# Second SAGE layer: one-hots loaded from HBM in place of made on VectorE, and stored there by the first

## The reference, cut to what matters

```
def _sage_conv(x, src, dst, Wl, Wr, b):
    msg = x[src]                                   # one row per edge
    agg = segment_sum(msg, dst)                    # summed by target node
    agg = agg / maximum(cnt, 1.0)
    return agg @ Wl.T + x @ Wr.T + b
h = relu(bn(sage_conv(x, src, dst, Wl0, Wr0, b0))) # first layer  (layer 0)
h = bn(sage_conv(h, src, dst, Wl1, Wr1, b1))       # second layer (layer 1)
x = layernorm(x + h)
```

## Time and profile before

| What | us |
|---|---|
| median of 3 runs (lowest 9302.91, highest 9314.57) | 9308.34 |
| span of the profiled execution, first to last instruction | 7890.3 |
| median less span | 1418.0 |
| layer 0 of SAGE, tile loop, 5421 to 6579 in the span | 1158 |
| layer 1 of SAGE, tile loop, 6684 to 7887 in the span | 1203 |

### The profile page before, as it was taken

One profiled execution on the slowest core, in us unless ns is written; L12 is line 12 of the kernel. 1 busy time (PEld: TensorE's weight loads), 2 busy tenths in 40 slices (PEclk: granted clock), 3 DMA queues, 4 the chain that ended last, 5 costly groups with the idle time before them and its releaser, 6 DMA issues.

```text
span 7890.3 us, 195306 instructions
## 1 busy us (share of the span) xinstructions
PE 5464.8 (69%) x50500; PEld 3952.8 (50%) x50501; DVE 4825.2 (61%) x14588; ACT 3085.2 (39%) x7615; POOL 5124.5 (65%) x4726
## 2 busy tenths in 40 slices
PE   3767677777773746777776777435878874888887
PEld 3655556565651336666666666323444442444444
DVE  7555555555556556666666666575666663555555
ACT  2111111111121135555555555413555552666665
POOL 1776767676740157777777777025887784777777
PEclk9977675656555855555555555567999996999999
DMA  3223232323233532222222222033555553544444
GB/s 122 57 56 77 56 77 56 77 56 77 56 76 125 148 47 52 52 51 51 51 51 51 51 51 51 12 91 95 124 124 125 124 125 92 120 116 118 118 118 107
DMA packets 600102, 647.29 MB, mean 82 GB/s; under 512 B 331121, under 2 KB 490355, under 8 KB 599665
## 3 DMA queue, kind: packets, MB, share of 16 engines
q0 software_dynamic: 190000, 384.58, 23.9%
q1 hardware_dynamic: 338379, 238.04, 10.4%
q10 hardware_dynamic: 71640, 23.81, 1.2%
HBM read 562.39 MB, written 83.23 MB: 82 GB/s over the span
## 4 chain that ended last, share of the span: by engine, by line
DVE 27%; issue 19%; POOL 15%; DMA 14%; PE 13%; DVEq 5%; ACT 3%; SPq 3%; ACTq 1%; POOLq 0%
POOL acc L659 8%; POOL rows L639 7%; DMA acc<-list_dst 7%; PE psa L1407 4%; PE psc L1366 3%; DMA rows<-t_gat,idx 2%; DVE acc L1729 2%; DVE acc L1781 1%; DMA acc<-in_x 1%; DVEq L619 1%; DMA acc<-y_d 1%; DVE acc L1728 1%; ACT ohb L1120 1%; PE psc L1498 1%; DVE s_m L1837 1%
## 5 line engine op out<-in xcount | busy, mean ns | idle before, releaser
L639 POOL DMA_INDIRECT rows<-t_gat,idx x3168 | 3142.8, 992 | 1189.8 <-issue 903.3
L659 POOL DMA_INDIRECT acc<-t_part,acc x1400 | 1826.6, 1305 | 546.6 <-issue 460.2
L1407 PE MATMUL psa<-rhs,rows 128*128 128x176 f32 (+1 forms) x6336 | 1713.1, 431 | 23.2 <-DVEq L1922 12.2
L1217 ACT ACTIVATE acc<-psa 128x384 bf16<-128x384 f32 x3200 | 1290.2, 506 | 884.7 <-PE psa L1481 765.8
L1407 PEld LDWEIGHTS psa<-rhs,rows 128*128 128x128 f32 x6336 | 1497.2, 311 | 132.0 <-DVEq L1922 83.2
L1481 PE MATMUL psa<-den,rhs 125*32 125x384 bf16 x12800 | 785.2, 343 | 191.4 <-ACT acc L1217 149.8
L1128 ACT ACTIVATE wgt<-s_d 128x64 f32<-128x64 f32 (+1 forms) x396 | 93.8, 237 | 1625.5 <-DVE s_d L1838 1610.8
L1122 ACT ACTIVATE oht<-psc 22x1024 bf16<-22x1024 bf16 x402 | 407.3, 1013 | 783.9 <-PE psc L1366 730.4
L1395 PE MATMUL psc<-oh,wgt 128*8 128x22 f32 (+1 forms) x6336 | 290.2, 205 | 552.1 <-ACT wgt L1128 543.8
L1071 ACT ACTIVATE acc<-stg,acc 128x128 bf16<-128x128 f32 x1818 | 552.9, 387 | 198.2 <-issue 116.0
L1481 PEld LDWEIGHTS psa<-den,rhs 125*32 125x32 bf16 x12800 | 285.6, 97 | 641.9 <-ACT acc L1217 412.7
(11 more groups left out here) (348 smaller groups left out, 7870.4 us busy)
## 6 DMA issues: line engine op xcount, KB each, us to landing
rows<-list_src SPq DMA_DIRECT2D x200, 500.0 KB
rows<-t_gat,idx POOLq DMA_INDIRECT x3168
acc<-y_d SPq DMA_DIRECT2D x50, 1000.0 KB, 5.0
y_d<-stg SPq DMA_DIRECT2D x100, 250.0 KB, 2.8
acc<-t_part,acc POOLq DMA_INDIRECT x1400
acc<-t_sage SPq DMA_DIRECT2D x300, 62.5 KB
adw<-win_d SPq DMA_DIRECT2D x820, 2.2 KB
adw<-win_d SPq DMA_DIRECT2D x788, 0.4 KB
```

The source lines that it names most:

```text
L639: eng.indirect_dma_start(rows[:, j, 0:spec["width"]], None, spec["table"], bass.IndirectOffsetOnAxis(ap=idx[:, j:j + 1], axis=0)).then_inc ...
L659: eng.indirect_dma_start(h_prow[u][:, t, :], None, t_parts[layer], bass.IndirectOffsetOnAxis(ap=h_idx[u][:, t:t + 1], axis=0)).then_inc(h_ ...
L1217: eng.activation(h_rows[:, g, :], psa[:, g % 4, 0:D3], ACT.Copy).then_inc(hyb["ev"], 1)
L1407: last = eng.matmul(sums(half, q, h), rows[:, slot * TH + j, 0:D], right, start=(j == 2 * q), stop=(j == 2 * q + 1))
```

## The change

Two tensors are added in HBM, one row per tile: `onehots_d` (128 x 2875 bf16, 736,000 bytes a tile) and `fetches_d` (125 x 2048 bf16, 512,000 bytes a tile).

- In layer 0 DVE makes both one-hots as before. SP stores `oh_src` of tile t after `lists(t)` and ahead of `own(t-1)` (`fetches_out`, after a wait for `sources(t)`), and `oh_dst` of tile t-1 after `own(t-1)` (`onehots_out`). DVE waits for the store of tile k-2 to be over before it writes the same buffer again.
- In layer 1 DVE makes neither (`targets` and `sources` are not called). SP loads `oh_src` from `fetches_d` in place of `list_src`, once the gathers of tile t-2 are done on PE; it loads no `list_dst`; after `list_idx` it loads `oh_dst` from `onehots_d`, once the segment sums of tile t-2 are done. PE waits for the loads where it waited for DVE.
- SP waits at each layer's end for the moves to be over.

```diff
@@ -188,6 +188,8 @@
         list_src = dram("list_src", (NT, GP * EP), BF16)
         list_dst = dram("list_dst", (NT, EP, GT), BF16)
         list_idx = dram("list_idx", (NT, EP, TP), I32)
+        onehots_d = dram("onehots_d", (NT, EP, GT * NP_), BF16)
+        fetches_d = dram("fetches_d", (NT, NP_, GP * EP), BF16)
         win0_d = dram("win0_d", (NW, 3 * K0), BF16)
         win1_d = dram("win1_d", (NW, 3 * K1), BF16)
         bnd0_d = dram("bnd0_d", (NP_, NT * H))
@@ -479,6 +481,9 @@
                          ("turn", "at", "ht", "mps", "used"))
         h_in = {k: [sem(f"h_{k}_in{u}") for u in range(2)] for k in ("lists", "idx", "own", "rows")}
         h_out = [sem(f"h_out{u}") for u in range(2)]
+        oh_moved = [n_msg[f"in{u}"] for u in range(2)]
+        src_moved = [n_bn[f"in{u}"] for u in range(2)]
+        moved_before = [16 * ((NC + 1 - u) // 2) for u in range(2)]
         act_l = sem("act_l")
 
         block = ctx.enter_context(nc.Block())
@@ -583,6 +588,14 @@
                     step(i * 2, t)
             for t in range(4):
                 step(NT - 2, t)
+
+        def onehots_of(e, k):
+
+            return onehots_d[ds(e + k, 1), :, :].rearrange("o p n -> p (o n)")
+
+        def fetches_of(e, k):
+
+            return fetches_d[ds(e + k, 1), :, :].rearrange("o p n -> p (o n)")
 
         def there(e, k):
             return not isinstance(e, int) or 0 <= e + k < NT
@@ -893,17 +906,40 @@
 
             def lists(e, k):
                 u, before, n = k % 2, later(e, k), e + n0
-                if before:
-                    eng.wait_ge(hyb["ohs"], n + (k - 1))
-                eng.dma_start(h_src[u], list_src[ds(e + k, 1), :].to_broadcast([NP_, EP * GP])).then_inc(h_in["lists"][u], 16)
-                if before:
-                    eng.wait_ge(hyb["ohd"], n + (k - 1))
-                eng.dma_start(h_dst[u][:, 0:GT], list_dst[ds(e + k, 1), :, :].rearrange("o p t -> p (o t)")
-                              ).then_inc(h_in["lists"][u], 16)
+                if layer:
+                    if before:
+                        eng.wait_ge(hyb["gps"], n * GP + (k - 1) * GP)
+                    eng.dma_start(oh_src[u].rearrange("p g s -> p (g s)"), fetches_of(e, k)).then_inc(src_moved[u], 16)
+                else:
+                    if before:
+                        eng.wait_ge(hyb["ohs"], n + (k - 1))
+                    eng.dma_start(h_src[u], list_src[ds(e + k, 1), :].to_broadcast([NP_, EP * GP])
+                                  ).then_inc(h_in["lists"][u], 16)
+                if not layer:
+                    if before:
+                        eng.wait_ge(hyb["ohd"], n + (k - 1))
+                    eng.dma_start(h_dst[u][:, 0:GT], list_dst[ds(e + k, 1), :, :].rearrange("o p t -> p (o t)")
+                                  ).then_inc(h_in["lists"][u], 16)
                 if before:
                     eng.wait_ge(h_in["rows"][u], n * (8 * TP) + 16 * TP * (k // 2))
                 eng.dma_start(h_idx[u][:, :], list_idx[ds(e + k, 1), :, :].rearrange("o p t -> p (o t)")
                               ).then_inc(h_in["idx"][u], 16)
+
+            def onehots_in(e, k):
+                u = k % 2
+                if later(e, k):
+                    eng.wait_ge(hyb["seg"], e + (n0 + k - 1))
+                eng.dma_start(oh_dst[u].rearrange("p g n -> p (g n)"), onehots_of(e, k)).then_inc(oh_moved[u], 16)
+
+            def fetches_out(e, k):
+                u = k % 2
+                eng.wait_ge(hyb["ohs"], e + (k + 1))
+                eng.dma_start(fetches_of(e, k), oh_src[u].rearrange("p g s -> p (g s)")).then_inc(src_moved[u], 16)
+
+            def onehots_out(e, k):
+                u = k % 2
+                eng.wait_ge(hyb["ohd"], e + (k + 1))
+                eng.dma_start(onehots_of(e, k), oh_dst[u].rearrange("p g n -> p (g n)")).then_inc(oh_moved[u], 16)
 
             def own(e, k):
                 u = k % 2
@@ -916,8 +952,14 @@
             def step(e, t):
                 if there(e, t):
                     lists(e, t)
+                    if layer:
+                        onehots_in(e, t)
+                    else:
+                        fetches_out(e, t)
                 if there(e, t - 1):
                     own(e, t - 1)
+                    if not layer:
+                        onehots_out(e, t - 1)
             return step
 
         def sp_node(eng, S, first, second=None):
@@ -1045,6 +1087,10 @@
                 eng.wait_ge(sp_in, 16 * n_in[0])
                 phase_end(eng, 9 + 2 * layer)
                 by_step(eng, sp_step(eng, layer))
+                for u in range(2):
+                    for moved in (oh_moved, src_moved):
+                        eng.wait_ge(moved[u], moved_before[u] + (layer + 1) * 16 * (NT // 2))
+                        eng.sem_inc(alone, 1)
                 phase_end(eng, 10 + 2 * layer)
 
 
@@ -1473,7 +1519,9 @@
 
             def gather(e, k, g):
                 u, n = k % 2, e + n0
-                if g == 0:
+                if g == 0 and layer:
+                    eng.wait_ge(src_moved[u], e * 8 + (moved_before[u] + 16 * (NT // 2) + 16 * (k // 2 + 1)))
+                if g == 0 and not layer:
                     eng.wait_ge(hyb["ohs"], n + (k + 1))
                 if g >= 4 or there(e, k - 1):
                     eng.wait_ge(hyb["ev"], n * GP + (k * GP + g - 3))
@@ -1486,7 +1534,10 @@
             def segment(e, k, g):
                 u, n = k % 2, e + n0
                 if g == 0:
-                    eng.wait_ge(hyb["ohd"], n + (k + 1))
+                    if layer:
+                        eng.wait_ge(oh_moved[u], e * 8 + (moved_before[u] + 16 * (NT // 2) + 16 * (k // 2 + 1)))
+                    else:
+                        eng.wait_ge(hyb["ohd"], n + (k + 1))
                     if later(e, k):
                         eng.wait_ge(hyb["comb"], n + (k - 1))
                         eng.sem_inc(alone, 1)
@@ -1972,9 +2023,10 @@
 
             def sources(e, k):
                 u, n = k % 2, e + n0
-                eng.wait_ge(h_in["lists"][u], n * 16 + 32 * (k // 2 + 1))
+                eng.wait_ge(h_in["lists"][u], e * 16 + 32 * (k // 2 + 1))
                 if later(e, k):
                     eng.wait_ge(hyb["gps"], n * GP + (k - 1) * GP)
+                    eng.wait_ge(src_moved[u], e * 8 + (moved_before[u] + 16 * (k // 2)))
                     eng.sem_inc(alone, 1)
                 eng.tensor_scalar(oh_src[u].rearrange("p g s -> p (g s)"), h_src[u], node1[:, 0:1], None,
                                   ALU.is_equal).then_inc(hyb["ohs"], 1)
@@ -1986,6 +2038,7 @@
                 link(tt(h_dstm[:, 0:GT], h_dst[u][:, 0:GT], dst_off[:, 0:1].to_broadcast([EP, GT]), ALU.add))
                 if later(e, k):
                     eng.wait_ge(hyb["seg"], n + (k - 1))
+                    eng.wait_ge(oh_moved[u], e * 8 + (moved_before[u] + 16 * (k // 2)))
                     eng.sem_inc(alone, 1)
                 link(tt(oh_dst[u], iota1[:, 0:NP_].unsqueeze(1).to_broadcast([EP, GT, NP_]),
                         h_dstm[:, 0:GT].unsqueeze(2).to_broadcast([EP, GT, NP_]), ALU.is_equal))
@@ -2047,11 +2100,11 @@
                 link.end()
 
             def step(e, t):
-                if there(e, t):
+                if there(e, t) and not layer:
                     targets(e, t)
                 if there(e, t - 2):
                     turned(e, t - 2)
-                if there(e, t + 1):
+                if there(e, t + 1) and not layer:
                     sources(e, t + 1)
                 if there(e, t - 2):
                     centre(e, t - 2)
@@ -2059,7 +2112,8 @@
                         scale(e, t - 2)
                 if there(e, t - 1):
                     combine(e, t - 1)
-            sources(0, 0)
+            if not layer:
+                sources(0, 0)
             return step
 
         @block.vector
```

## The result

The changed kernel takes 10352.16 us against 9312.49 us, medians of 5 runs each: 1.112 times as long, interval 1.1106 to 1.1133, +1040 us. Forecast were 9690 us and a range up to 9960. The sign is right, the size is not.

The account below looks back on a forecast made before the run. It took each tile loop to be paced by a chain through SP's list loads and DVE's one-hots, with POOL nearly equal in layer 0. Layer 0 +502 us and layer 1 -121 us gave +381, so 9690 us, range 9440 to 9960.

Parts of the forecast that it names:

- What was shown as the base: Whole kernel: a traced span of 7890.3 us with 1418.0 us more around it, kept unchanged, from a median of 9308.34.
- Two covers go with L1990: Layer 1, targets' one-hots no longer made on DVE: PE's 0.9 us wait for `turned` and the lengthened POOL gather end.
- without it POOL needs 7 x 1.25 = 8.75 us a tile and is no bound: Layer 1: with no DVE operation stretching a gather from 0.95 to 3.15 us, POOL's seven gathers don't set the pace.
- the two stores: Layer 0, SP's queue: storing `oh_src` costs 3.85 us on five engines, storing `oh_dst` 1.73 us, ahead of the next list.
- The queue's 9.91: Layer 0, one round on SP's queue: `oh_src` store 3.85, own rows 0.48, `oh_dst` store 1.73, source list 3.85 us.
- the packets of POOL and ACT: Layer 0: other transfers sharing the DMA engines add 4.3 us to the round, between 3.0 and 5.5.
- No gain in layer 1: Rival: `oh_src` load takes the list's place, nothing won; layer 1 at 11.9 to 12.5 us, 9797 to 9856; chance 0.15.
- cheaper stores: Rival: 125-partition stores use all engines or packets fit gaps; layer 0 at 12.8 to 14.5 us, 9307 to 9473; chance 0.12.
- hidden: Rival: stores are hidden, POOL paces layer 0 at 11.58 us, only the -121 us remains, 9187; chance 0.06.
- stretched: Rival: other engines' packets grow in proportion to the transfers; layer 0 at 19.3 us a tile, 9944 in all; chance 0.12.
- the signs named: Layer 0 loop some 1660 us, DVE awaiting lists 5 us; layer 1 some 1080, POOL's mean about 0.95, PE awaiting loads.

Follow-up runs that it names:

- e0: The kernel before, unchanged, run again on a 7900 chip: 7904.8 us, ratio 1.001.
- h0: The kernel before, unchanged, one run on a 9200 chip for a trace: 9206.7 us against 9168.3.
- g2: Changed kernel, but layer 1 loads only the sources' one-hots and makes the targets' on DVE; 9200 chip: 9669.3 us, 1.055 times the kernel before.
- t1: Changed kernel, sources' one-hots split 112/13, layer 0 stores behind the next loads, useless DVE operation in layer 1; 9200 chip: 9189.9 us, 1.003.
- h1: The changed kernel, unchanged, beside the kernel before on a 9200 chip: 10222.4 us, ratio 1.115.
- g1: Changed kernel, but layer 1 loads only the targets' one-hots and makes the sources' on DVE; 9200 chip: 10220.6 us, 1.115 times the kernel before.
- e3: The changed kernel, unchanged, beside the kernel before on a 9200 chip: 10359.7 us, ratio 1.113.
- e6: Changed kernel, sources' one-hots moved as 112 and 13 partitions, both layer 0 stores behind the next tile's list loads; 9200 chip: 9881.0 us, 1.062.
- e4: Changed kernel with the sources' one-hots stored and loaded as 112 and 13 partitions; 9200 chip: 10115.7 us, 1.087 times the kernel before.
- e5: Changed kernel with both layer 0 stores of a tile behind the next tile's list loads; 9200 chip: 9922.4 us, 1.067 times the kernel before.
- s1: The changed kernel, unchanged, beside the kernel before on a 7900 chip: 8462.3 us, ratio 1.071.
- g3: Changed kernel with six of the seven GpSimd gathers of layer 1 left out; 7900 chip: 8285.0 us, 1.049 times the kernel before.

## Why the prediction was right in part and wrong in size

- **What was shown as the base: wrong.** "The trace's execution has a span of 7890.3 and the runs have 1418.0 more around it, which I leave as it is, for want of a row on it." Nothing lies around the span: the profiled execution of e0 took 7907 us with a span of 7905, that of h0 9207 with 9205. The difference is inside: between the trace of before and h0 the spans differ by 1314 us, of which 1056 lie ahead of the loops (5421 against 6477) and 280 in them (2361 against 2641 us); the stretch between the loops is 20 us shorter. Carrying the 1418 us along did no harm by itself, since they stand on both sides. The harm is that every row of the prediction comes from one sort of chip and the result from the other.
- **Layer 1: the step that failed, and nearly all of the error.** Forecast 10.8 us a tile, -121 us; measured 11.1 to 11.2 on 7900 chips (a gain of 65 us) and 18.1 to 18.2 on 9200 chips, (18.10 - 12.67) x 99 = +538 us. The failed step is "Two covers go with L1990", above all "without it POOL needs 7 x 1.25 = 8.75 us a tile and is no bound". POOL's mean did fall to 0.95 us. But on a 9200 chip layer 1 takes 12.6 to 12.7 us where a DVE operation stalls GpSimd in its row (h0, g2, t1) and 18.0 to 18.4 where none does (h1, g1, e3 to e6), with the loads the same in t1 and e6. The end of an interference was booked as a gain, and the tile lost 5.4 us by it. No row of the base could have shown this; that it was counted as safe on one trace is the fault.
- **Layer 0: right in mechanism, 1 us a tile short.** Forecast 16.7 us, measured 17.65 on both sorts (11 traces, 17.64 to 17.68). On a 7900 chip that is (17.65 - 11.47) x 99 = +612 us where +502 was forecast; on a 9200 chip, which starts from 12.95, +465. The terms that were mis-sized are the two stores. On each of the engines that they use, the packets of the store of `oh_src` take 5.5 us where 3.85 stood, those of `oh_dst` 2.6 where 1.73 stood; the list takes 4.0 for 3.85, the own rows 0.7 for 0.48 (medians and means of layer 0 of the changed kernel; five and sixteen engines). The queue's 9.91 are 12.8, which leaves 2.4 us for the packets of POOL and ACT, where 4.3 stood. That the sum came within 1 us owes something to these two errors having opposite signs. A packet's time may hold some waiting for others, so the split between the two is as near as the trace gets. The five engines (e4) and the place in the queue (e5) are both shown. The Trainium skill ("DMA: Bandwidth & Descriptors", "Why a DMA increments its semaphore by 16 and not by 1") has a DMA use the largest number of engines up to 16 that divides the slowest dimension; e4 agrees: 112 and 13 partitions in place of 125 take 2.4 us a tile away.
- The sum on the chips of the result: +465 and +538 make 1003 of the 1022 us by which the spans of h1 and h0 differ (10227.0 and 9204.8); the rest lies outside the two tile periods. On a 7900 chip +612 and -65 make 547 of the 561 us measured (s1), where +381 was forecast. So the forecast was too low there as well, by both layers.
- **Rivals.** "No gain in layer 1", "cheaper stores" and "hidden" are out; "stretched" (19.3 us in layer 0) is too high by 1.65. The stores are dearer than read, not cheaper. The hidden case is out as argued: the list waits behind the stores in SP's one queue. None of the rivals had layer 1 slower than 12.5 us. Of the signs named, those of layer 0 came; in layer 1 POOL's mean fell as named, and PE waits for the load of `oh_src` on a 7900 chip (s1, 170.9 us over 59 tiles from 7310 to 8460), but for neither load on a 9200 chip.
- **The granted clock** in layer 1 of the result is 0.72, in s1 0.92 and in t1 0.91. It is low where PE stands idle in gaps: t1, on the slower sort of chip, has it back with the gaps gone. PE was busy 12.8 us a tile at 0.72 and 9.6 at 0.92, so the clock may add to the loss once the gaps are there; no run takes the two apart.

**Still open.** That the loads don't cost on a 9200 chip and the missing DVE operation does is shown. How is read from the traces: signals between engines are recorded late while GpSimd issues gathers without a break. Why they are late, and why on one sort of chip alone, isn't shown, and the recorded changes of semaphores have gaps in the traces of 9200 chips, so single ones prove little. That it takes the stall of GpSimd, and not just a long operation on DVE, is argued: a DVE operation as long that stalls no gather wasn't tried. Neither was pacing on a 9200 chip, the direct way to break the row, nor g3 there. No chip stands in two groups, so "sort of chip" could also be a condition that a chip was in at the time.

## What to carry to other kernels

When the profiled span and the timed runs differ by 15%, ask first whether they are of the same machine; don't put the difference "around" the span. A transfer put into a queue costs what is queued behind it: the same bytes, behind the next tile's loads in place of ahead of them (e5), cost 4.2 us a tile less. And an engine that stalls another isn't always a cost: look at what gets done during the stall before removing it.

## What was not expected of the hardware

- The same kernel takes 7893 to 7902 us on three chips and 9168 to 9303 on three others. Waits put down to "remote" exist on the second sort alone. Three of them in the kernel before (h0), all stages:

```profile
ACT oht L1122 <- remote: 1537.3, 262, 11.2
DVE pen L1834 <- remote: 904.8, 192, 37.3
...
DVE acc L2000 <- remote: 347.0, 98, 14.2
```

  The trace of the same kernel on a 7900 chip (e0) has no such row. Where GpSimd issues few gathers or none the two sorts agree: the first 192 us of the kernel before, with 6 gathers, take the same in e0 and h0, and so does a stretch of 81 us with none (from 2344 and from 2896 us). The stretch between them, with some 1600 gathers, takes 2153 us in e0 and 2704 in h0.
- On a 9200 chip a useless DVE operation of 2.3 us made a loop 5.7 us a tile shorter.
- A signal between engines can be late: the transposes' semaphore changes a median of 5.97 us after their end in the changed kernel on a 9200 chip, 0.01 us on a 7900 chip (s1).
- The Trainium skill ("SBUF — State Buffer", "Who interferes with whom") states that GpSimd and VectorE share one pair of ports as an exclusive lock, and that PE and ACT never wait on anyone. The 2.05 us gather beside L2051 agrees with the first part. The second is on ports; the 3.12 us that ACT waits in the row of gathers above end with a semaphore, so it doesn't cover them.
